# An attention, scan and binary-weight tower on one core: the first norm folded into two projections, with a new order of steps

## The reference, cut to what matters

```python
x = emb[inp]
q = x @ Wq.T + bq;  k = x @ Wk.T + bk;  v = x @ Wv.T + bv     # split into 16 heads
attn = softmax(q @ k.T * scale);  ctx = attn @ v              # joined again: 256 features
h = ctx @ Wo.T + bo

n = layernorm(h)                       # (h - mean) / sqrt(var + eps), no weight or bias
Bu_proj = (n @ B_w.T) @ C_w.T
s = blelloch_exclusive_scan(a=sigmoid(log_decay), b=Bu_proj)
gate = sigmoid(n @ gate_w.T + gate_b)
h = h + gate * s

h = h + layernorm(h) @ sign(weight).T
```

## Time and profile before

| | before |
|---|---|
| median of 3 runs | 702.97 us (701.63 to 703.03) |
| profiled execution, its time | 703.16 us |
| its span, first to last instruction | 701.4 us |
| outside the span | 1.8 us |
| TensorE busy | 647.6 us, 92% of the span |
| ScalarE busy | 606.9 us, 87% |
| VectorE busy | 577.8 us, 82% |
| GpSimd busy | 407.8 us, 58% |

### The profile page before, as it was taken

The page is one execution under the profiler, slowest core; times in us unless marked ns, Lnnn a source line. Parts: engine busy times, 40 slices in busy tenths (PEclk is TensorE's granted clock), DMA queues, the critical chain, the costliest instruction groups (busy, mean ns, idle before and its releaser), DMA issues. The chain is left out here.

```text
span 701.4 us, 21283 instructions
## 1 busy us (share of the span) xinstructions
PE 647.6 (92%) x6727; PEld 611.2 (87%) x6727; DVE 577.8 (82%) x1205; ACT 606.9 (87%) x2249; POOL 407.8 (58%) x463
## 2 busy tenths in 40 slices
PE   3578999999999999999999999999999999998863
PEld 2468899999999999999999999999999999998752
DVE  3456788888989898888998998888998998888742
ACT  2398999999999999999999999999999999999510
POOL 7410466765655666765655666776565565655552
PEclk9799999999999999999999999999999999999975
DMA  6323333223333333223333333233333333222000
GB/s 155 109 92 106 107 107 90 90 94 109 119 120 105 120 120 99 85 95 101 113 120 105 120 120 116 77 95 96 109 120 119 105 120 120 88 75 79 17 16 30
DMA packets 56161, 69.81 MB, mean 100 GB/s; under 512 B 6784, under 2 KB 41792, under 8 KB 56128
## 3 DMA queue, kind: packets, MB, share of 16 engines
q1 hardware_dynamic: 52048, 60.48, 25.1%
q0 software_dynamic: 3072, 8.39, 6.0%
q10 hardware_dynamic: 1008, 0.53, 0.4%
HBM read 10.65 MB, written 8.39 MB: 27 GB/s over the span
## 5 line engine op out<-in xcount | busy, mean ns | idle before, releaser
L392 ACT ACTIVATE probs<-ps_s,neg_max 128x128 f32<-128x128 f32 x1024 | 346.5, 409 | 36.5 <-DVE neg_max L527 36.4
L527 DVE TENSOR_REDUCE neg_max<-ps_s 128x4 f32<-128x512 f32 x256 | 175.9, 687 | 39.1 <-PE ps_s L676 30.2
L748 PE MATMUL ps_t<-ident,probs 128*128 128x128 f32 x1024 | 158.8, 278 | 11.8 <-ACT probsT L402 10.8
L402 ACT COPY probsT<-ps_t 128x512 f32<-128x512 f32 x256 | 165.9, 648 | 1.6 <-PE ps_t L748 1.6
L392 ACT ACTIVATION_READ_ACCUMULATOR probs<-ps_s,neg_max 128x1 f32 x640 | 146.7, 229 | 0.0
L748 PEld LDWEIGHTS ps_t<-ident,probs 128*128 128x128 f32 x1024 | 113.9, 141 | 36.7 <-issue 25.1
L676 PE MATMUL ps_s<-k_stack,q_stack 128*128 128x256 f32 x512 | 124.5, 324 | 6.1 <-DMA q_stack<-q_low 6.0
L318 POOL TENSOR_TENSOR state_high<-state_in,ones_col 128x512 fp32r<-128x512 f32 x32 | 33.3, 1040 | 163.5 <-DVE state_in L663 163.5
L304 POOL TENSOR_TENSOR xn<-h,mv 128x512 f32<-128x512 f32 x64 | 66.8, 1044 | 63.5 <-DVE ve L554 62.9
L560 DVE TENSOR_REDUCE row_sum<-probs 128x4 f32<-128x512 f32 x96 | 65.3, 680 | 28.3 <-ACT probs L392 28.3
L676 PEld LDWEIGHTS ps_s<-k_stack,q_stack 128*128 128x128 f32 x512 | 77.9, 192 | 7.2 <-DMA q_stack<-q_low 7.2
(11 more groups left out here) (120 smaller groups left out, 1886.9 us busy)
## 6 DMA issues: line engine op xcount, KB each, us to landing
k_stack<-k_high SPq DMA_DIRECT2D x128, 128.0 KB, 2.5
q_stack<-q_high SPq DMA_DIRECT2D x64, 256.0 KB, 2.4
k_stack<-k_low SPq DMA_DIRECT2D x64, 128.0 KB, 2.3
q_stack<-q_low SPq DMA_DIRECT2D x32, 256.0 KB, 2.5
out<-y SPq DMA_DIRECT2D x32, 256.0 KB, 2.1
x_emb<-in_emb,id_col POOLq DMA_INDIRECT x64, 3.7
raw<-in_wkT SPq DMA_DIRECT2D x1, 256.0 KB, 3.2
raw<-in_wqT SPq DMA_DIRECT2D x1, 256.0 KB, 4.2
```

Source lines behind the costliest of these rows:

```text
L392: last = nc.scalar.activation(probs[s % 2][:, j], ps_s[s % 2][:, j * SEQ:j * SEQ + SEQ], ACT.Exp, bias=neg_max[s % 2][:, j:j + 1], accum_o ...
L402: nc.scalar.copy(probsT[st][vp if st < AHEAD else 0][:], ps_t[:]).then_inc(act_pT, 1)
L527: nc.vector.tensor_reduce(neg_max[s % 2][:], ps_s[s % 2][:].rearrange("p (h k) -> p h k", h=HPS), axis=AX.X, op=ALU.max, negate=True).then ...
L748: last = nc.tensor.transpose(ps_t[:, j * SEQ:j * SEQ + SEQ], probs[st % 2][:, j], ident[:])
```

## The change

The first norm is no longer made as a tensor. With `h0 = ctx @ Wo.T + bo`, the norm is `rs * (h0 - mean)`, and subtracting the mean is linear: it is put into centred copies of `Wo` and `bo` that are made once, at the start. The kernel then multiplies the centred `Wo` by the gate's weight and by the state's (at the start, on TensorE in plain fp32: six turns, twelve matmuls), and in the turns the gate and state projections read `ctxT` in place of `xn1T`. What is left of the norm is the factor `rs1` for each token, with two rows that come from `bo`: `state_mid` is state plus `state_row`, `state_in` is `state_mid * rs1 * powers_tok`, `gate_in` is gate times `rs1` plus `gate_bias`, and GpSimd makes `gate_bias = gate_row * rs1 + gb_row`. Of the first norm go out, in each turn: four turns on TensorE, the copy `xn1Th` on ScalarE, the subtraction `xn1Tl` on VectorE and two passes on GpSimd. In come `state_mid` and two passes on GpSimd, and `gate_in` and `state_in` become two instructions of 256 columns each.

The order in the turn is changed too: the output projection goes from slot 7 to slot 6, the state projection from slot 6 to slot 1 (ahead of turning the embeddings), the sign projection ahead of `attention(0)`, the scan's matmuls from slot 1 to slot 7 of the turn before; `k_high` and `k_low` go one slot ahead; the split of the state goes to the end of the turn before on GpSimd. `ve` becomes a sum of two columns, of which one holds eps.

The diff, cut to its core:

```diff
 # GpSimd, one turn
+                    scale(t - 2, ve1, rs1, rs1_done)
...
+                    nc.gpsimd.tensor_tensor(gate_bias[:], gate_row[:].unsqueeze(1).to_broadcast([P, 2, D]),
+                                            rs1[:].unsqueeze(2).to_broadcast([P, 2, D]), ALU.mult).then_inc(bias_step, 1)
+                    nc.gpsimd.tensor_tensor(gate_bias[:], gate_bias[:], gb_row[:].unsqueeze(1).to_broadcast([P, 2, D]),
+                                            ALU.add).then_inc(pool_bias, 1)
 # VectorE
-                    nc.vector.tensor_scalar(ve[:], mv[:, :, 1], EPS, None, ALU.add).then_inc(done_ve, 1)
+                    nc.vector.tensor_tensor(ve[:], mv[:, :, 1], eps_col[:], ALU.add).then_inc(done_ve, 1)
 # VectorE, slot 2
+                    nc.vector.tensor_tensor(state_mid[:], g0[:].rearrange("p (b d) -> p b d", b=2),
+                                            state_row[:].unsqueeze(1).to_broadcast([P, 2, D]), ALU.add).then_inc(dve_mid, 1)
 # VectorE, slot 3, behind norm_moments and v_wide
+                    for b in range(2):
+                        last = nc.vector.scalar_tensor_tensor(state_in[:, b], state_mid[:, b], rs1[:, b:b + 1], powers_tok[:],
+                                                              ALU.mult, ALU.mult)
+                    last.then_inc(dve_in, 1)
+                if exists(t + 1):
+                    split_low(k_low, g3, bk_col, k_high, act_khi, dve_klo)
 # VectorE, slot 6
+                    for b in range(2):
+                        last = nc.vector.scalar_tensor_tensor(gate_in[:, b], g1[:, b * D:b * D + D], rs1[:, b:b + 1],
+                                                              gate_bias[:, b], ALU.mult, ALU.add)
 # TensorE, at the start
+                for dst, row, src in ((ps_c, 0, raw[1]), (g2, D, ws_raw)):
+                    for c in range(C):
+                        for k in range(C):
+                            mm(dst[:, c * D:c * D + D], wo_turned[:, k, c * P:c * P + P], src[:, k], k == 0, k == C - 1)
+                    for k in range(C):
+                        last = mm(g3[:, row:row + D], bo_turned[:, k, 0:P], src[:, k], k == 0, k == C - 1)
+                last.then_inc(fold_made, 1)
 # TensorE, slots 6 and 7
                 attention(6)
-                if exists(t - 2):
-                    await_first((dve_qlo, C, t + 1, C), (dve_gated, 1, t - 3, 1))
-                    token_major(g0, ws, xn1T, PARTS, pe_state)
-
-                attention(7)
                 if exists(t - 3):
                     await_event(pe, pool_xn2, 1, t - 3, 1)
...
                     to_features(g3, lambda b: xn2[:, b], pe_xn2T)
                 if exists(t - 1):
                     await_event(pe, dve_ctxlo, 1, t - 1, 1)
                     token_major(g2, wo, ctxT, PARTS, pe_o)
+                attention(7)
+                if exists(t - 2):
+                    await_event(pe, state_lows, 1, t - 2, 1)
```

More of the change, by code:

```diff
@@ L124, in build @@
         rs1, rs2 = sb("rs1", [P, 2]), sb("rs2", [P, 2])
-        xn1, xn2 = sb("xn1", [P, 2, D]), sb("xn2", [P, 2, D])
+        xn2 = sb("xn2", [P, 2, D])
         gate_in, gate_tanh = sb("gate_in", [P, 2, D]), sb("gate_tanh", [P, 2, D])
-        state_in = sb("state_in", [P, 2, D])
+        state_mid, state_in = sb("state_mid", [P, 2, D]), sb("state_in", [P, 2, D])
+        gate_row, state_row = sb("gate_row", [P, D]), sb("state_row", [P, D])
+        gate_bias = sb("gate_bias", [P, 2, D])
+        row_mean = sb("row_mean", [P, C + 1])
         state_high, state_low = (sb(f"state_{n}", [P, 2, D], f32r) for n in ("high", "low"))
         gated = sb("gated", [P, 2, D])
+        wo_cent, bo_cent, wo_turned, bo_turned, ws_raw = xn2, gated[:, 0], gate_in, gate_tanh, state_mid
         y = [sb(f"y{p}", [P, 2, D]) for p in range(2)]
@@ L437, in turn @@
                     for c in range(C):
[L438 removed]
+                        nc.scalar.activation(k_high[:, c], g3[:, c * 256:c * 256 + 256], ACT.Identity,
                                              bias=bk_col[:, c:c + 1]).then_inc(act_khi, 1)
+                exponentials(3)
                 move_probsT(4)
[L441 removed]
                 move_inverse(t - 1)
```

249 lines of the change are left out of this document (140 added, 109 removed).

## The result

| | before | after |
|---|---|---|
| median of 4 runs | 702.35 us (701.63 to 703.03) | 720.91 us (718.38 to 722.26) |
| ratio, 95% interval | | 1.026 (1.0226 to 1.0295) |
| profiled execution, its time | 703.16 us | 722.26 us |
| its span | 701.4 us | 720.5 us |
| a turn in the middle, from the starts of `h0` | 19.63 us | 20.19 us |

The change made the kernel 2.6% slower. The forecast was 711 us with a range of 690 to 724: the sign and the range held, but of a loss of 19.1 us in the profiled execution it gave 8.

A forecast was written before the change was run, and what follows sets the result against it. The prediction took the loop through VectorE's list, ctxTl and the output projection, lengthened by a GpSimd collision, to bound the changed kernel: 703.16 + 10.1 (turns) + 2 (start) - 4 (end) = 711 us, range 690 to 724.

The forecast's parts named there:

- Steps 1 and 2: Turn: TensorE alone would need about 19.25 us, but waits 0.8 for VectorE's list before the output projection; turn 19.7.
- Rivals B: Loop through VectorE's list without a collision with GpSimd: turn 19.7, 702 us (697 to 706); chance 0.26.
- C: TensorE stays the bound, VectorE getting through its list sooner: turn 19.25, 689 us; chance 0.18.
- Step 3: VectorE's state_in waits for GpSimd's subtraction for xn2: 0.34 us a turn, bounds nothing and 0.34 + 0.57.
- rival D: Worse collision: state_in's second half waits for the power, or ctxTl meets the state's split; 727 us; chance 0.13.
- A's own: Main case, the loop through VectorE's list plus the state_in collision: 711 us, 705 to 719; chance 0.43.
- D's second condition: VectorE's ctxTl meets GpSimd's split of the state at the end of its turn: up to a pass of 1.05.
- Step 4: Sum of a turn: 8.3 + 0.34 + 11.4 = 20.04 against 19.68, +0.36; +10.1 us over 28 turns.
- Step 5: Removed xn1 copy and subtraction, new ve, gate_bias on GpSimd and the moved state split: all costed at nothing.
- Step 6: Start: twelve plain fp32 matmuls ahead of the first scores cost between 0 and +3.4 us, taken as +2.
- Step 7: End, last h0 to last y: shorter chain for the last pair, -4 us, bounds -6.5 and -1.

The follow-up runs named there:

- e12: Changed kernel with both VectorE-GpSimd meetings ordered apart, k_high behind the exponentials of step 3, maxima(4) ahead of k_low, v_wide left in slot 3: ratio 1.043.
- e9: Changed kernel with both VectorE-GpSimd meetings taken apart by order and the scan's matmuls moved behind attention(0) of the next turn: ratio 1.033.
- e2: Changed kernel in which GpSimd waits for state_in before starting the subtraction for xn2: 723.57 us, ratio 1.030.
- e13: Changed kernel with GpSimd's gathers of the embeddings moved behind the split of the state: ratio 1.016.
- e4: Changed kernel with ve again in its form from before the change, a scalar addition of eps: 723.67 us, ratio 1.028.
- e10: Changed kernel without meetings, scan's matmuls moved, v_wide in slot 2, k_high behind exponentials(3), maxima(4) ahead of k_low: ratio 1.030.
- e16: As e10, with the gathers behind the split of the state and the row sums of step 5 behind xn2Tl: 699.86 us, ratio 0.995.
- e3: Changed kernel with the output projection back behind attention(7): 729.32 us, ratio 1.038.
- e5: Changed kernel with v_wide moved into slot 2 on VectorE: 727.30 us, ratio 1.024.
- e15: As e10, with the gathers behind the split of the state, and sums(5) and xn2Tl ahead of gate_in: ratio 1.023.
- e18: As e16, with the gathers back in the changed kernel's place, ahead of the split: 723.65 us, ratio 1.031.

## Why the prediction was right in its sign and wrong in its size

**Steps 1 and 2 (the loop through VectorE's list and W).** Right as a mechanism, and in size: from W to the next S3 pass 11.34 us (11.4 said), TensorE waits for `ctxTl`. The list without meetings is as long as said: in e12 `ctxTl` starts at 7.43, for 7.58 said, of which 0.13 is `ve`. ScalarE's chain, which I gave no relief but no weight either, was there at S3 + 7.3 for T6, and in the changed order it holds W at 8.43 or 8.44 even without a meeting (e9, e2). Rivals B (no meeting) and C (TensorE stays the bound) are refuted.

**Step 3 (the meeting).** The meeting itself is right: 0.41 a turn for 0.34 said, inside its bounds. The `ve` ahead of it cost 0.13 less than its row gave. But this is the step that failed, by what it left out: the second meeting, of `ctxTl` with the split of the state, stands at nothing in the sum, and only as a condition of rival D, with the whole at 0.13. It costs `ctxTl` 0.32 in nearly every turn. e13 shows what it was worth: with the split ahead of `ctxTl` the turn is 19.88 in place of 20.19. The place could have been read: `ctxTl` at S3 + 7.9, and GpSimd's new list adds up from `ve` to the split at about 7.0 (an estimate from GpSimd's distances between starts in the kernel before; measured 7.2), so the two passes of the split end at 9.3 or so, behind the start of `ctxTl`. The measured time lies as this says: above A's own 705 to 719, at the low end of D's 719 to 735, with D's second condition met and not its first.

**Step 4 (the sum of a turn).** Here the omission comes out as a number: from S3 to W 8.64 said, 8.89 measured (+0.32 for the second meeting, +0.07 for the first, -0.13 for `ve`), and from W to S3 11.4 said, 11.3 measured. So 20.04 against 19.68 said, +0.36; measured 20.19 against 19.63, +0.56. Over 28 turns that is 15.7 us for 10.1. The other three distances bring it to 19.1 over all 31: the first turns grow by more (20.67 and 20.3 between the second and the fourth `h0`, for 19.73 and 19.63), and the last distance is 14.96 for 13.27. VectorE's timeline of the changed kernel, the first `h0`, and the last with the last `y`:

```profile
70.22 0.68 DVE L631 TENSOR_TENSOR h<-ps_g,bo_row 128x512 f32<-128x512 f32 x1
```

```profile
690.21 0.69 DVE L631 TENSOR_TENSOR h<-ps_g,bo_row 128x512 f32<-128x512 f32 x1 [0.95 <-PE ps_g L724]
...
717.22 0.69 DVE L646 TENSOR_TENSOR y<-ps_g,h 128x512 f32<-128x512 f32 x1 [2.17 <-PE ps_g L724]
```

(620.0 us there, 600.9 before, from 67.2 to the earlier trace rows.)

**Step 5 (costed at nothing).** Right for `ve` (e4). Missing from it are three moves that cost little or nothing visible only because VectorE's list hid them: `k_high` ahead of exponentials that were ready, `maxima(4)` behind `k_low`, and the gathers, whose DMAs I had not looked at. e9 and e10 have no meeting, and their turn is 20.33 and 20.23. In e9 the first two still hold W at 8.43. In e10 they are mended and W is at 8.04, but 0.38 goes to the stacking DMAs and 0.42 to the sign projection's wait for `xn2Tl`.

**Step 6 (start).** +3.0 from the first `h0`, for +2, inside its bounds, but the size was luck. Eight of the fold's matmuls took 3.46 us from 24.31 on in the changed kernel, and 1.89 in e16, which has the same fold, behind idle times of 2.59 and 2.69 us. The windows of 2 us there (granted clock in the third column from the end) are, of the changed kernel and of e16:

```profile
24.00:26.00 2.00, 2.00 (x6) 1.66 (x7) 1.57 (x3) 0.00 (x0) 1.15 (x3) 0.52 0.82 263
26.00:28.00 2.00, 2.00 (x7) 1.66 (x6) 0.00 (x0) 0.00 (x0) 0.00 (x0) 0.63 0.71 270
```

```profile
24.00:26.00 2.00, 2.00 (x11) 1.77 (x10) 1.14 (x3) 0.00 (x0) 1.44 (x3) 1.00 0.90 246
```

In the changed kernel these windows are a mixture of the two levels, nearer to 1.2 GHz; in e16 it is 2.4 GHz. All profiled kernels with the whole fold fall into two sets: where the eight matmuls took 1.89 (e3, e5, e13, e15 to e18), 7.70 us pass from the first of the eight to the first maxima; where they took 3.02 to 3.62 (the changed kernel and ten others), 8.83 to 10.50 do, 9.27 in the changed kernel. So the clock is worth 1.6 us of its start, and my row of four matmuls said nothing on which of the two it would be. In e13, which differs from the changed kernel only in the gathers, the first `h0` is at 67.78, 0.6 behind the kernel before.

**Step 7 (end).** 27.0 us from the last `h0` to the last `y`, so -3.0 for -4, inside its bounds.

Sum, in the profiled executions: +19.1 + 3.0 - 3.0 = 19.1 us; said +10.1 + 2 - 4.
